# Twelve blocks of maxima leave the first group of attention and are made in the three groups behind it

## The reference

```python
qkv = jnp.einsum('btc,oc->bto', x, w_attn)          # then 32 heads of 16, rope on q and k
scores = jnp.einsum('bhqd,bhkd->bhqk', q, k) / jnp.sqrt(16)
scores = jnp.where(causal, scores, -jnp.inf)
attn = jax.nn.softmax(scores, axis=-1)
y = jnp.einsum('bhqk,bhkd->bhqd', attn, v)          # plus a small adapter of 10 tokens
x = x + layernorm(y @ w_proj.T)
x = x + layernorm((silu(x1 @ W_gate.T) * (x1 @ W_up.T)) @ W_down.T)   # x1 = layernorm(x)
```

## Time and profile before

| | |
|---|---|
| median of 3 runs | 1179.44 us (1171.9 to 1182.09) |
| the profiled execution | 1173.92 us |
| its span, first to last instruction | 1172.1 us |
| PE busy | 1096.0 us, 94% |
| DVE busy | 700.5 us, 60% |
| ACT busy | 501.3 us, 43% |

### The profile page before, as it was taken

One profiled execution on the slowest core, in us unless ns is written; L12 is line 12 of the kernel. 1 busy time (PEld: TensorE's weight loads), 2 busy tenths in 40 slices (PEclk: granted clock), 3 DMA queues, 4 the chain that ended last, 5 costly groups with the idle time before them and its releaser, 6 DMA issues. The chain is left out here.

```text
span 1172.1 us, 18100 instructions
## 1 busy us (share of the span) xinstructions
PE 1096.0 (94%) x7020; PEld 752.9 (64%) x7020; DVE 700.5 (60%) x973; ACT 501.3 (43%) x1054; POOL 262.9 (22%) x257
## 2 busy tenths in 40 slices
PE   5999999898999999999999988899999999999996
PEld 4778778543445555555545544677887887887884
DVE  5756746776778888878887764573525224325113
ACT  3324232334777777777777755124321121121110
POOL 6624538201311111111111133451001001001001
PEclk9999999757999999999999998999999999999998
DMA  7456776641444444444443323644313003002000
GB/s 253 129 147 171 166 181 179 128 102 38 80 80 85 90 88 90 90 89 92 88 81 95 127 86 117 202 144 149 110 52 108 1 1 108 1 1 67 6 1 36
DMA packets 93917, 113.08 MB, mean 96 GB/s; under 512 B 26504, under 2 KB 54792, under 8 KB 93832
## 3 DMA queue, kind: packets, MB, share of 16 engines
q1 hardware_dynamic: 91768, 108.07, 35.9%
q10 hardware_dynamic: 2064, 3.85, 2.0%
HBM read 68.82 MB, written 42.21 MB: 95 GB/s over the span
## 5 line engine op out<-in xcount | busy, mean ns | idle before, releaser
L882 ACT ACTIVATE prob<-ps_s 128x512 f32<-128x512 f32 (+3 forms) x768 | 323.7, 496 | 173.3 <-PE ps_s L1032 166.8
L906 DVE TENSOR_REDUCE neg<-ps_m 128x2 f32<-128x1024 f32 (+2 forms) x224 | 248.3, 1145 | 58.5 <-PE ps_m L997 36.2
L1032 PE MATMUL ps_s<-q_op,k_op 50*128 50x512 f32 (+2 forms) x768 | 242.6, 449 | 18.0 <-ACT prob L882 13.5
L997 PE MATMUL ps_m<-k_op,q_op 48*128 48x512 f32 (+2 forms) x768 | 186.4, 423 | 9.9 <-DVE neg L906 7.1
L1032 PEld LDWEIGHTS ps_s<-q_op,k_op 50*128 50x128 f32 x768 | 117.5, 192 | 119.6 <-ACT prob L882 61.8
L840 POOL TENSOR_SCALAR_AFFINE_SELECT prob<-prob 128x512 f32<-128x512 f32 x128 | 83.3, 651 | 396.3 <-ACT prob L882 396.3
L1046 PE MATMUL ps_y<-prob,vg 128*17 128x512 f32 (+3 forms) x1536 | 150.5, 512 | 0.0
L1618 DVE TENSOR_TENSOR hf<-sl,ps_u 128x512 f32<-128x512 f32 (+1 forms) x44 | 30.2, 686 | 173.1 <-PE ps_u L78 152.1
L906 DVE TENSOR_REDUCE neg_far<-ps_m 128x4 f32<-128x512 f32 (+2 forms) x96 | 100.3, 1048 | 31.0 <-PE ps_m L1002 29.6
L997 PEld LDWEIGHTS ps_m<-k_op,q_op 48*128 48x128 f32 x768 | 97.4, 199 | 29.7 <-DVE neg L906 20.4
L1683 PE MATMUL ps_d<-w_high,wp_high 128*128 128x512 f32 (+1 forms) x352 | 115.1, 389 | 0.0
(11 more groups left out here) (176 smaller groups left out, 1699.3 us busy)
## 6 DMA issues: line engine op xcount, KB each, us to landing
y_heads<-y_sb SPq DMA_DIRECT2D x32, 256.0 KB, 2.1
raw<-in_w_ffn SPq DMA_DIRECT2D x31, 256.0 KB, 3.2
k_op<-k_parts SPq DMA_DIRECT2D x28, 256.0 KB, 4.6
q_op<-q_parts SPq DMA_DIRECT2D x56, 128.0 KB, 5.1
v_groups<-v_out SPq DMA_DIRECT2D x16, 272.0 KB, 4.1
q_parts<-part_h SPq DMA_DIRECT2D x16, 256.0 KB, 2.9
q_parts<-part_l SPq DMA_DIRECT2D x16, 256.0 KB, 2.9
k_parts<-part_h SPq DMA_DIRECT2D x16, 256.0 KB, 2.9
```

Source lines behind the costliest of these rows:

```text
L882: act.activation(prob[:, v % NPROB, h, unit_cols(u)], ps_s[:, y % NS, unit_cols(u)], ACT.Exp, scale=D ** -0.5).then_inc(s_exp, 1)
L906: nc.vector.tensor_reduce(to[:, :, pairs[0]:pairs[-1] + 1, i - TT * c], scores, axis=AX.X, op=ALU.max, negate=True).then_inc(a_read, 1)
L997: last = nc.tensor.matmul(ps_m[:, g % 2, s, base:base + wide], q_op[buf][r, c, pair, (i - TT * c) * P:(i - TT * c + 1) * P], k_op[buf][r, ...
L1032: nc.tensor.matmul(ps_s[:, y % NS, lo:BLK], k_op[buf][r, pair, j * P:(j + 1) * P], q_op[buf][r, c, pair, lo:BLK], start=True, stop=True)\
```

## The change

`ramp_pattern` makes a string for groups 1, 2 and 3 (`RAMP` = 3): `PATTERN` with one more M behind the 6th, 8th, 12th and 23rd S (`RAMP_AT`), 26 in place of 22. `first_pattern` gets 12 less for the part behind the 8th S, so that group 0 has 33 M in place of 45. From group 4 on all is as it was, as is everything ahead of group 0's 9th S. The diff:

```diff
--- before.py
+++ after.py
@@ -47,6 +47,8 @@
 TURN = 3
 LEAD = 11
 LAG = 4
+RAMP = 3
+RAMP_AT = (6, 8, 12, 23)
 PATTERN = "SMPPSMPPSMSMSMSSMSSMSMPPSMMSSMMSPPMSMSMSMSMPPSMMSPPMSMSMSS"
 
 
@@ -664,6 +666,17 @@
     return out + "M" * (behind - behind * (pairs - half - 1) // (pairs - half))
 
 
+def ramp_pattern():
+
+    out, pairs = "", 0
+    for step in PATTERN:
+        out += step
+        pairs += step == "S"
+        if step == "S" and pairs in RAMP_AT:
+            out += "M"
+    return out
+
+
 def stage_attention(nc, block, ctx, semctx, passed, d, ident, projection, place, start, masks_of, operands, op_sems, last_block, done, tail):
 
     (inv_const, max_in, a_ps, a_read, m_step, m_high, m_ready, s_ps, s_exp, masked, pv, pv_zero,
@@ -685,11 +698,12 @@
     early = {tt: range(2 * tt - 2, 2 * tt) for tt in range(1, TT)}
     first_main = at[(0, "turn", 0)] + 5
     half_main = at[(0, "turn", 1)] + 5
-    first_steps = first_pattern(half_main - first_main, at[(2, LEAD)] - half_main)
+    first_steps = first_pattern(half_main - first_main, at[(2, LEAD)] - half_main - RAMP * len(RAMP_AT))
+    ramp_steps = ramp_pattern()
 
     def steps(n):
 
-        return PATTERN if n else first_steps
+        return first_steps if n == 0 else ramp_steps if n <= RAMP else PATTERN
 
     taken = {}
     unit = -LAG
```

## The result

The changed kernel takes 1188.01 us (median of 8 runs, 1183.77 to 1193.48) and the one before 1180.36 us (8 runs, 1171.9 to 1182.34). The ratio is 1.0077, with a 95% interval of 1.005 to 1.0103: slower, by less than 1%. Only that it stays within 1% of before, which had 0.7, came true. The profiled execution took 1183.77 us, 9.9 us more than the one before.

The account below looks back on a forecast made before the run. TensorE at half clock, then VectorE's blocks, bound group 0; the fixed S, M, P order sets ordinary groups. Terms -11.4 + 8.1 = -3.3 us gave 1176 us (from the 1179.44 median), range 1164 to 1188.

Parts of the forecast that it names:

- Group 0's gain: Behind group 0's 8th S: twelve M fewer there save 11.4 us, with ends of 4.8 and 13.7 us.
- early recovery: Rival: group 0's half clock ends some 20 us sooner, worth 9 us, for 1167 us; chance 0.19.
- VectorE's term: Groups 1 to 3: four M more each cost 2.7 us per group, 8.1 us in all, ends 0 and 12.5.
- I set both to zero in the sum: Clock in groups 1 to 3: more falls from added waits, fewer from those removed in group 0, both counted as nothing.
- The prediction's own sign: Groups 1 to 3: a clock below 0.85 there would show the forecast wrong.
- The slower rival: Groups 1 to 3, 3rd to 9th S: TensorE waits for VectorE, the clock falls, 1192.6 us; chance 0.11.
- The price from group 11: A 1.74 us reciprocal between two blocks lengthened group 11 by 1.14 us: 65% of added VectorE time is paid.
- The late turn: Group 1's c = 1 turn moves behind its 3rd S; the 9th S waits for its DMAs: nothing, up to 1 us.
- SyncE's queue: Group 0's last store and group 4's load wait until group 1's 10th S; both needed a group later: no cost.

Follow-up runs that it names:

- h3: Kernel before, with the causal mask matmuls left out of the maxima of groups 6 to 13, 64 per group; 1202.72 us, ratio 1.0189.
- h4: Kernel before, with extra VectorE reductions into a spare tile (three in group 4, four each in 5 and 6, one in 7); 1191.71 us, ratio 1.01.
- e1: The change, with the four M more of groups 1 to 3 behind S 1, 2, 10 and 18; runs 1181.45, 1187.49, 1205.19 and 1207.18 us.
- f4: The change, with all twelve M moved into group 1 and the old places from group 2 on; 1178.78 us, ratio 1.0019 to before.
- e2: The change, with the score matmuls of groups 1 to 3's blocks of maxima issued twice; 1188.71 us, ratio 1.0087 to before.
- f2: Kernel before, with the score matmuls of all blocks of groups 2 to 13 issued twice; 1202.21 us, ratio 1.0227.
- e4: The change, with the string of 26 M in groups 4 to 6 and the old string of 22 M in groups 1 to 3; 1213.65 us, ratio 1.0307 to before.
- f1: Kernel before, with LEAD 7 for 11: five M fewer in group 0, blocks five places later in groups 1 to 12; 1205.67 us, ratio 1.0278.
- f3: Kernel before, with LEAD 7 for 11 and the score matmuls of all blocks of groups 2 to 13 issued twice; 1224.32 us, ratio 1.0426.
- h1: Kernel before, with six M moved from group 0 into group 1 and the old places from group 2 on; 1176.39 us, ratio 0.9961.
- h2: The change with all twelve M in group 1, and the score matmuls of that group's 34 M issued twice; 1177.4 us, ratio 0.9971 to before.

## Why the prediction was wrong

- **Group 0's gain** was right in size: 12.6 us between the two profiled executions, for 11.4 forecast. In the seven traces with 33 M in group 0 it took 48.9 to 50.8 us, and in the three with the old group 0 (before, h3, h4) 62.0, 60.9 and 60.4; between the means lie 11.3 us. Half clock ended sooner than the 269.24 us of before, first at 246.50 and again at 260.15, as the busy times of the changed kernel by stretches of one clock have it:

```profile
246.50:249.91 3.41, 3.12 (x15) 1.59 (x13) 2.89 (x5) 2.85 (x6) 0.00 (x0) 1.00 0.00 0
249.91:260.15 10.24, 10.24 (x52) 4.16 (x50) 5.87 (x5) 6.03 (x12) 0.64 (x1) 0.50 0.69 122
260.15:269.91 9.76, 9.22 (x110) 5.24 (x114) 7.09 (x9) 5.98 (x15) 1.91 (x3) 1.00 0.52 94
```

  The means of 0.63 and 0.58 make it 36 us at half clock in place of 52. So an early recovery did come and is inside the 12.6 us, which the forecast had reached without one: part of that match is luck. The first rise isn't the change's doing either. h3 and h4 had it too, 25 us behind the start of their old group 0, and e1 and f4, whose group 0 is the changed one, didn't have it.
- **Groups 1 to 3, VectorE's term**: 8.1 us forecast, some 9.2 by the estimate from e2 and f2, the shift's small own part (0.7 to 0.9 us a group in e4, f1 and f3) among it. As a sum this was right. The split was not: by h4 four reductions at the old places cost 0.9 us beside the clock, not 2.7. In f4 twelve M cost 40.36 - 29.81 = 10.6 us, 3.3 of them the clock: 0.6 us each.
- **The step that failed is "I set both to zero in the sum"**, of the clock in groups 1 to 3. It came to 12.7 to 13.0 us by two estimates (9.4 by the lowest price), as much as the whole gain. Without it the sum is -12.6 + 9.2 = -3.4 us, which is the forecast; with it, groups 0 to 3 are 9.5 us longer. The profiled executions lie 9.9 us apart and the medians 7.7. The prediction's own sign, a clock below 0.85 in groups 1 to 3, showed in group 1 (0.77).
- Why I set it so: I read that groups 4 to 13 hold the clock "in the same order with only four M fewer". They were not the same order. The prediction itself says that each later M comes twelve, eight and four places later, and I took that as bookkeeping; it moved the mask matmuls out of the one stretch that needs them (e4, f1, h3). Nor would zero have held without a shift: VectorE's added time alone brought falls (h4).
- **The slower rival** had the right place, the right sign and the right price per us at half clock. It asked for 46 us at half clock, and there were 37.6, so its 1192.6 us was too much: the loss stayed under its 1%. Its chance of 0.11 was too small. Its mechanism, TensorE waiting for VectorE, fits the change's first fall and not those of f1. The Trainium skill's rule in "TensorE: Matmul & The Clock Gate", section "A second HAM failure mode: psum-queue depth-cycling", that short idle times between groups of matmuls which cycle through PSUM banks make the clock fall and rise, stood beside this rival. The change's first fall agrees with it, with waits of 0.30 to 0.51 us between blocks from 276.67 us on; f1's falls show no such waits for VectorE, with TensorE busy for 4.01 of 4.22 us.
- **The price from group 11** The earlier trace rows was read where the clock had held. In the changed kernel's profile the same reciprocal in the same order came with a clock of 0.85 and 33.08 us, 3.5 more, and in e4's and h1's too; in e1, e2, f4 and h2 it took 29.5 to 29.6 us. A price read from one trace is one of two there. This fall, which the change doesn't cause by its order, is in the 9.9 us between the two profiled executions.
- **The late turn** at no cost was right; so was SyncE's queue, since nothing in groups 1 to 3 waited for a DMA.

## What to carry to other kernels

When work is moved in a hand-made interleaving, follow what moves behind it: a string of slots that is filled from a list fits one phase of the list, and a shift by a few entries changes every slot until it is taken back. Here taking it back in the next group (f4, h1) was better than over three. And count anything that thins out TensorE's matmuls, waits in short pauses or work left out, as a risk for its clock, not as free room: in this kernel the same VectorE work cost some 0.9 us by waits and 4.7 us by the clock (h4).

## What the runs showed of the hardware

- Leaving 64 small mask matmuls out of a group made it 2.3 to 5.9 us longer (h3), while TensorE's clock fell to its lower level, 1.2 GHz, two or three times in each; issuing matmuls twice raised the mean clock of the change's groups from 0.77 to 0.95, 0.87 to 0.91 and 0.86 to 1.00 (e2).
- A us at half clock cost 0.46 us in groups 1 and 2 of the kernel before, 0.47 in single falls elsewhere and 0.34 in group 11 of the change; 0.46 fits the change (12.7 us worked out, 13.0 by e2 and f2).
- A group that repeats exactly can repeat its fall to 0.02 us (9.14 to 9.16 us behind the start in groups 2 to 10 of f1). At other places the same order falls in one execution and not in the next: group 11, and group 0's rise.
- The busy time of TensorE doesn't tell where the clock falls: it fell behind 5.26 us busy of 5.62 (f1) and held at 5.42 of 5.90 (before, group 4).
- The same order with doubled matmuls held the clock for four groups and then lost it (f3), which stays open.
